# Masking the second attention behind its exponential on GpSimd, and a new order of steps

## The reference

```
x = x + L0_attention(norm(x), ctx)          # 16 heads of 16, softmax, no mask
x = x + L0_ffn(norm(x))                     # one of 8 experts, chosen by a gate
x = x + L1_attention(norm(x), ctx)          # 16 heads of 16, with cantor_mask:
    mask = cantor_mask(S, 7, 64)            # fixed pattern, 256 x 256, the same for all heads
    scores = q @ k.T * SCALE
    scores = where(mask, scores, finfo.min)
    attn = softmax(scores); out = (attn @ v) @ Wo + bo
x = x + L1_ffn ... L2_attention ... L2_ffn ... L3_attention ... L3_ffn
```

## Time and profile before

| | |
|---|---|
| runs | 987.82, 987.9, 988.53 us; median 987.9 |
| profiled execution, first to last instruction | 986.1 us |
| median of the runs less this span | 1.8 us |
| TensorE | busy 949.3 us (96%), mean granted clock 0.993 |
| VectorE | busy 634.1 us (64%) |
| ScalarE | busy 536.3 us (54%) |
| GpSimd | busy 221.5 us (22%) |

### The profile page before, as it was taken

How to read it: one execution, slowest core, us unless ns; L and a number is a source line. 1 busy time by engine, 2 the same in 40 slices (tenths; PEclk the granted TensorE clock), 3 DMA queues, 4 the chain that set the end, 5 groups by cost and what they waited for, 6 DMA issues and landing times.

```text
span 986.1 us, 17493 instructions
## 1 busy us (share of the span) xinstructions
PE 949.3 (96%) x6126; PEld 702.7 (71%) x6126; DVE 634.1 (64%) x2245; ACT 536.3 (54%) x1097; POOL 221.5 (22%) x317
## 2 busy tenths in 40 slices
PE   8999999989999999999999999999999999999998
PEld 6665665757687766778687766776686757777777
DVE  4634674675675776867586776775776676736564
ACT  1341644776368643875448644866376544864421
POOL 3104311303240132403141023302321032012210
PEclk9999999999999999999999999999999999999999
DMA  7308535400540023520432104402132004000000
GB/s 261 58 30 226 127 113 113 88 10 17 113 94 9 11 50 70 113 49 13 80 73 46 44 1 86 98 11 49 27 67 59 12 17 92 1 12 1 1 1 22
DMA packets 41078, 58.27 MB, mean 59 GB/s; under 512 B 4096, under 2 KB 35840, under 8 KB 37376
## 3 DMA queue, kind: packets, MB, share of 16 engines
q1 hardware_dynamic: 39600, 48.59, 23.6%
q10 hardware_dynamic: 1392, 8.56, 2.3%
HBM read 41.67 MB, written 13.89 MB: 56 GB/s over the span
## 4 chain that ended last, share of the span: by engine, by line
PE 77%; ACT 9%; DVE 8%; issue 4%; POOL 1%; DMA 1%; ACTq 0%; SPq 0%; DVEq 0%; POOLq 0%
PE bank L1657 11%; PE bank L1984 6%; PE bank L1517 6%; PE bank L1736 6%; PE bank L1714 6%; PE bank L1508 6%; PE bank L1629 4%; PE bank L1995 4%; PE bank L1771 4%; PE bank L1765 3%; PE bank L1717 3%; ACT PT L886 2%; ACT QA L873 2%; PE bank L1797 2%; PE bank L1526 2%
## 5 line engine op out<-in xcount | busy, mean ns | idle before, releaser
L886 ACT ACTIVATE PT<-bank 128x512 f32<-128x512 f32 x256 | 153.0, 598 | 127.4 <-PE bank L1717 71.8
L1657 PE MATMUL bank<-w,xhT 128*128 128x512 f32 x256 | 126.8, 599 | 0.0
L1714 PE MATMUL bank<-QA,KA 104*128 104x256 bf16 x512 | 112.7, 273 | 12.4 <-ACT PT L886 10.5
L1184 DVE CUSTOM_DVE_ANT_0 bank<-bank,maskb 128x256 f32<-128x256 f32 x256 | 101.7, 450 | 25.7 <-PE bank L1629 25.4
L1177 DVE TENSOR_REDUCE mx<-bank 128x2 f32<-128x512 f32 x128 | 83.6, 684 | 28.9 <-PE bank L1629 28.5
L1629 PE MATMUL bank<-KA,QA 96*128 96x256 bf16 x512 | 91.1, 273 | 1.9 <-DVE mx L1184 0.8
L1984 PE MATMUL bank<-xhBT,wi 128*128 128x256 f32 x336 | 87.0, 390 | 2.9 <-DVE hT L1491 2.5
L1714 PEld LDWEIGHTS bank<-QA,KA 104*128 104x128 bf16 x512 | 46.5, 99 | 60.3 <-issue 45.8
L1230 DVE SCALAR_TENSOR_TENSOR x<-bank,one,x 128x256 f32<-128x256 f32 x128 | 61.5, 481 | 21.6 <-PE bank L1657 17.6
L873 ACT COPY QA<-bank 8x256 bf16<-8x256 bf16 (+1 forms) x128 | 67.8, 575 | 10.1 <-PE bank L1695 8.8
L1984 PEld LDWEIGHTS bank<-xhBT,wi 128*128 128x128 f32 x336 | 59.2, 191 | 12.9 <-DVE hT L1491 5.6
(11 more groups left out here) (311 smaller groups left out, 2028.3 us busy)
## 6 DMA issues: line engine op xcount, KB each, us to landing
QA<-scratch SPq DMA_DIRECT2D x90, 128.0 KB, 4.8
scratch<-kparts SPq DMA_DIRECT2D x30, 192.0 KB, 2.4
KA<-scratch SPq DMA_DIRECT2D x15, 384.0 KB, 4.6
scratch<-qparts SPq DMA_DIRECT2D x30, 192.0 KB, 2.3
KA<-scratch SPq DMA_DIRECT2D x15, 256.0 KB, 5.5
w<-pack ACTq DMA_DIRECT2D x1, 2345.0 KB, 8.3
wi<-ipack ACTq DMA_DIRECT2D x1, 2304.0 KB, 8.5
xin<-x_in SPq DMA_DIRECT2D x8, 256.0 KB, 6.3
```

Of the source, the lines that this page charges most:

```text
L886: act.activation(PT[:, n % RING, :, :].rearrange("p t s -> p (t s)"), st_bank[:, :], ACT.Exp).then_inc(exp_s, 1)
L1184: last = dve.tensor_tensor_reduce(s, s, maskb[:, t, :], op0=ALU.add, op1=ALU.max, scale=1.0, scalar=-HUGE, accum_out=mx[:, i % 4, n % GH, ...
L1657: last = pe.matmul(bank[n % 2][:, :], xhT[:, kk, t * P:(t + 1) * P], W("exp0", KT)[:, kk, i * 512:(i + 1) * 512], start=(kk == 0), stop=(k ...
L1714: last = pe.matmul(st_bank[:, t * S:(t + 1) * S], KA[m][0:KM, v, t * P:(t + 1) * P], QA[m][0:KM, v, :], start=True, stop=(m == 0))
```

## The change

The 256 matmuls of L1717 go. For m = 1 the exponential is taken of unmasked scores. A new thread `value` on GpSimd waits for each head's exponential, multiplies the bits of the 128x512 weights, read as int32, by a tile `keepb` of int32 0 or 1, in place, and signals `kept_s`; the product with the values waits for `kept_s` in place of `exp_s` for m = 1. DVE makes `keepb` once, by two more 128x256 instructions, beside `maskb`. All five strings of `TURNS` are new. Per thread each engine still has the same number of letters, but for 128 new `v` on GpSimd, `w` 106 to 185 and `z` 54 to 56 on TensorE.

```diff
 TURNS = {
...
     "gpsimd":
-        "ppppppppssppsppsppsssppspssppsppssappsspsssasppaapapbbppbsbpsabssppbapbsaappsapbsbbspbpssabbbppssppp"
-        "apsapssaabbpspbbsbbsappssppaspbpassaaspbbbbbppsbapsaspspsppsspabasabpbbpbpabsbsbssappssssaaapbpssbss"
-        "bbbabaaasbabaabaabbaabaaaabcccccccccccccbc",
+        "ppppppppppppsssspppsppspssvsvpssvvvvvvpvvvvpvvvvsppsassapspppppsvvssvavvvaavvbvvvvbvbvvvpspbsasbpsbp"
+        "spppbpapavvvavsavvsvvbsvbbvvvvvvvbpsabsbsppsppppbspapaasavvvvbsvsvvbvpvvbvvbvvbvvsbappppbsasspppspvv"
+        "avvavsasvvvbsvbvbvvbvpvvvbsspbapbasspspppppsssvvavavavvvvbvpvbvvvvvvbbasbsbsspbspsvvsvspavvavavpvabv"
+        "vvsvvvvsbvssbbbabvvbvvvvvvvvvvvsvvvaaaabaaabbabaaabaabaccccccbcccccccc",
...
     "tensor":
-        "pppwwwppwwwwwwwwwwwwwwwwppwwwwwwwwwwwwpwwwwwpwpwwwwwwppwwwwwwwwwwwwwwwwwwwsswwspspssvsvswwvsvpsvswwv"
-        "ssvpvvssvpsvwwwvvvvwwvpvvvvwwwvpvwwwvvwwwwvpvwwvpvvpwwwwwwwpwspsssssssssssssssssppbspsspbsspssbpssvb"
...
+        "pppwwppwwwwwwwwwwwwwwwwwwwwwwwwppwwwwwwpwwwwwwwwwwwwwwwwwwwwwwwwpwpwwwwwppwwwwwwwwwwwwwwwwwwwwwwwwww"
+        "wwwwwwwwwwwwwwwwwwwwwwwwwwwwwwsswwspspssvwsvssvsvpvsswsvswvpvvpvsswwvwwvvvvwwvwwwwwvvvvpvwwvpvvwwvpv"
+        "wwvwwvvpwwwwwwwwwwspsssssssssspspssssssppwwwwwwwpspsswwwwwwwsspsspssvbsvbsbvssvwwwwpssvbsvbvpvvsspvb"
+        "vbvsvvvwwvpwvvvvbvwwvpvvssvpsvsssvwssvssvsssspsvsvpvvwwvwpwsvpsvsvvsvssvssvvvvssvsvvsvvsvssvsvssvpvp"
...
 }
@@ -208,6 +210,7 @@
         ident = W("ident")
         identb = sb("identb", [P, P], BF16)
         maskb = sb("maskb", [P, T, S], BF16)
+        keepb = sb("keepb", [P, T, S], I32)
         bqs = [sb(f"bqs{m}", [P, KT]) for m in range(3)]
         hb4 = sb("hb4", [P, 1])
         hb3 = sb("hb3", [P, 1])
@@ -364,7 +367,7 @@
 
         s_ps, max_s = sem("s_ps"), sem("max_s")
         mq_s, mT_ps, negm_s = sem("mq_s"), sem("mT_ps"), sem("negm_s")
-        st_ps, exp_s = sem("st_ps"), sem("exp_s")
+        st_ps, exp_s, kept_s = sem("st_ps"), sem("exp_s"), sem("kept_s")
         pv_ps, ot_s, otT_ps, att_s = sem("pv_ps"), sem("ot_s"), sem("otT_ps"), sem("att_s")
         attT_ps, attT_s, o_ps, added = sem("attT_ps"), sem("attT_s"), sem("o_ps"), sem("added")
 
@@ -694,6 +697,17 @@
                     plus(xb1, x, "bo1", xb1_s)
                     yield
 
+            def value():
+                pool.wait_ge(mask_ready, 3)
+                for q, (b, m) in enumerate(ATTENTIONS):
+                    if m == 0:
+                        continue
+                    for n in range(q * H, (q + 1) * H):
+                        pool.wait_ge(exp_s, n + 1)
+                        pt = PT[:, n % RING, :, :].bitcast(I32)
+                        pool.tensor_tensor(pt, pt, keepb[:, :, :], ALU.mult).then_inc(kept_s, 1)
+                        yield
+
             def net():
                 pool.wait_ge(w_in[6], 16)
                 for b in range(B):
@@ -748,7 +762,7 @@
             for m in range(2):
                 link("p", pool.memset(vflat[m][:, :, H * VW:], 0.0))
                 pool.memset(vaug[m][:, :, :, HD:HD + 1], 1.0).then_inc(ones_ready, 1)
-            weave("gpsimd", prep(), score(), iter(()), net(), rest(stream), rest(final))
+            weave("gpsimd", prep(), score(), value(), net(), rest(stream), rest(final))
 
 
         @block.scalar
@@ -1266,7 +1280,8 @@
                 yield
                 dve.wait_ge(nomask_in, 16)
                 for t in range(T):
-                    last = dve.tensor_copy(maskb[:, t, :], att[:, t, :])
+                    dve.tensor_copy(maskb[:, t, :], att[:, t, :])
+                    last = dve.tensor_scalar(keepb[:, t, :], att[:, t, :], 0.0, None, ALU.is_ge)
                 last.then_inc(mask_ready, 1)
                 yield
                 for q, (b, m) in enumerate(ATTENTIONS):
@@ -1700,7 +1715,7 @@
                     if q == 0:
                         pe.wait_ge(mask_ready, 1)
                     elif (b, m) == (0, 1):
-                        pe.wait_ge(mask_ready, 3)
+                        pe.wait_ge(mask_ready, 2)
                     tops(q, 0)
                     yield
                     for v in range(H + 4):
@@ -1712,10 +1727,7 @@
                                 pe.wait_ge(exp_s, n)
                             for t in range(T):
                                 last = pe.matmul(st_bank[:, t * S:(t + 1) * S], KA[m][0:KM, v, t * P:(t + 1) * P],
-                                                 QA[m][0:KM, v, :], start=True, stop=(m == 0))
-                                if m == 1:
-                                    last = pe.matmul(st_bank[:, t * S:(t + 1) * S], identb[:, :], maskb[:, t, :],
-                                                     start=False, stop=True)
+                                                 QA[m][0:KM, v, :], start=True, stop=True)
                             last.then_inc(st_ps, 1)
                             yield
                             if v % GH == 1 and v // GH + 1 < ITEMS:
@@ -1731,7 +1743,10 @@
                                     pe.wait_ge(attT_s, q)
                             for g in (2 * pair, 2 * pair + 1):
                                 i = q * ITEMS + g
-                                pe.wait_ge(exp_s, GH * (i + 1))
+                                if m == 0:
+                                    pe.wait_ge(exp_s, GH * (i + 1))
+                                else:
+                                    pe.wait_ge(kept_s, b * H + GH * (g + 1))
                                 for t, h in itertools.product(range(T), range(GH)):
                                     last = pe.matmul(pv_bank[32 * h:32 * h + 32, g % 2 * S:(g % 2 + 1) * S], vflat[m][:, t, (g * GH + h) * VW:(g * GH + h) * VW + 32],
                                                      PT[:, (i * GH + h) % RING, t, :], start=(t == 0), stop=(t == T - 1),
```

More of the change, by code:

```diff
@@ L90 @@
     "sync":
-        "pppppppppppppppppsssppbspppppppppppspssppsppppppppppbsssppsppbpppppppppsppsbspsppbpppppppppppbspspsp"
-        "spbpppppppbpppsppspssbppppppppsbsppspspppbpppspsssbcbbcc",
+        "pppppbpppppppppppspspssppppppppppppppsspspsppppppppppsppsspsppbbpppppppppbsppspsspbppppppppbppspspss"
+        "pppppppppbppspsspppbspppppppbpspsppssbpppppbppcssssbbbcc",
     "gpsimd":
-        "ppppppppssppsppsppsssppspssppsppssappsspsssasppaapapbbppbsbpsabssppbapbsaappsapbsbbspbpssabbbppssppp"
@@ L97 @@
+        "vvsvvvvsbvssbbbabvvbvvvvvvvvvvvsvvvaaaabaaabbabaaabaabaccccccbcccccccc",
     "scalar":
-        "pppppppppppvvpvvvpvvvvvvpvvvvvvvvvvvpvpsspsppsbsbpvpvbvvvpvvvvvvpvvvvvvvvsvvvvpbpvbvbbvvvsvbvvvvbvbv"
-        "vvvvvvbbvbpvvvvbpsbpasbabavavabvvvpvavpvvvvaapvvvvvpvavbvbvavvapvapvaavsavvvvvvvvavbavvvvvvbvpbvvvvb"
-        "vppsbsabbavaabavbpvavvpbvabvvvvvbpavbvvvvabvvavvvavpavaaabvvvvvavavpvvvpvsvvbvbvvvvvbvvvbvpbbspapsab"
-        "avavabvvvpbvpvabvvvavbavpbvvvvbavavvvavpavaaavbpvpavvavvsvpvvvvbvbvvbvvvvvpvbvvbvbvpssbababpavpbavbv"
@@ new lines @@
+        "pppppppppppvvpvvvpvvvvvvpvvvvvvvvvvvpvspsspppsssvbvpbvpvvpvvbvvvvpbvbbvvvvvvvvbvbvvbppvvvvvbsbvvvpvv"
+        "vbbvvvvvbvbvbvvbbvvbppvssaappavavbavvvavvpvvvaaavpvavvvvvbvvvvavavpapvavsavvvvvvavvavpvvvvvbvvvbvvvb"
+        "ppvsbsabbaavavabvvavbppvabvapbvvvbvavpbvavvvvbvavvvvaavabavvvvpvavavpvvvsvvvbvvvbvvvbvvvbvbbpsppasba"
+        "avavbavvpvpabvpvabvvvbvaavbvvavvbvvavvpvavaavabpvpvavavvsvvpvvvbvbvvvvbvvvvpbvpvbvbvsbsababvappbavbv"
+        "vapvbvvvabvvvavvavvavabvpvavvvavavapavvpvvvvvavavvsvbvbvpvvvbvvvbvvbvbpvpssbababavavabvvvavpvpvvvpvb"
@@ new lines @@
+        "avbvvvvabavavvvavpvabavavavsvvvvvavvavvvvvvbvvbvvvpbvvvbpabbasaspbabvppavbvvvvbvavvvvbvvvvvbvavbvvap"
+        "avavvapvvbvvvavsvaaavvvvaavvvvvbvvvvbsvsvbvcbabbaavavbavvvbavvvbvvababavabvvvavvbvavavavabvvaavbaaba"
+        "aaabaaaaaaaaaaaaabaaaaaaaaaaabbaaaabcbccbcbccbbcbccccccccccccccccccc",
+    "vector":
+        "ppppppvppvvppppppssssssssssssssssssssvvpvvppvsssspsspssssssspssssssppssssssssssssbssvbvpsvsssvspssss"
+        "psssssvssssssspspsssssvvsssssvvsvaasppsssssspssssaaassssssssssssssssssavssaassssvpvsvspssspvsspaaasp"
+        "aasasaabsbvsbsbbsbvbsbbssvsvbbbvaabsssppssbsbsssbssaaapssbssbsssssbssbssssbssaaavsbsbvssvvsspssvaaaa"
+        "abpsasspssabsapbsbssbvbbbbbbvsbssbsbvsvbpssvsababbssssspsspsssbapaasssbsssbssbssssbssavbsaasssssvssb"
+        "ssvsvspssaaaspaavpsabsspababpsbbsbbbbbbsvssbbsbsvsbvsvsbbsbvapapsssbpssssbssbsssbssaaabssssbsssssssb"
+        "vssaaasssvsspvbvssspsvpsaaasaapassspbasabsbsbsbbbbbbsvsbbsbsbsvssvvsbbvabasssssbsspsssbssspaaabssssp"
+        "sssssbssbsssvsbsssvaaasssssbsvsvssvsbsaaaaasasbsasabpbvsbvbbbpbbbsspvbvbsbvaabsspspbbbsssssbssssssss"
+        "bsaaasssbssbspvbssbssssssvaasasvsvsbsssvsssssssssbaaaassasabssaabsbsvssbbbbbvbbpvvbbbvacabcsssssbsbs"
+        "sbsssaaasbsssbsbsbssasaabbvvbaaaaababvvaabvabaaabbbbbbbaaaabbbaaaabaaaaaaaaaabbaaabcacccbccccccbcccc"
+        "cbcccbcccccbcbccccccccccccccccccbcccc",
```

43 lines of the change are left out of this document (14 added, 29 removed).

## The result

The changed kernel takes 1067.4 us in the median of 4 runs, the kernel before 987.9: a ratio of 1.0805, 95% interval [1.0781, 1.0828]. The prediction said 976.5 and at most 991. It is wrong by 91 us and in its sign.

The account below looks back on a forecast made before the run. It took TensorE's queue to bound the stretch from attention 1 to 15, and step order the first 135 us. 986.1 + 11.5 + 1.0 - 28.2 + 5.0 (stalls) - 0.7 = 974.7 of span, plus 1.8 outside: 976.5 us; range 965 to 991.

Parts of the forecast that it names:

- The 56 surplus spins: Ahead of the first scores: added spins cost 12.2 us, 0.7 absorbed by idle time, so +11.5 (bounds 11.0 to 12.3).
- The 22 others: Attention 1's stretch: 22 added spins, 4.8 us against 3.8 us of idle, forecast +1 (bounds 0 to 4.8).
- The transfer into `QA`: Before the first scores: transfers had landed by 35.48 us, so the scores would not have waited for them anyway.
- The multiplication's duration: GpSimd's 128 integer products of 128x512: 1.17 us each taken from the nearest rows, 150 us in all.
- Its use in TensorE: Masked attentions, heads 4 to 7: waits for the product in six of eight, 6 x 0.12 = 0.7 us.
- rival B: Masked attentions: the GpSimd product is slow; at 2.33 us each, 60 us lost, about 1036 us. Chance 0.15.
- the lock: GpSimd holding DVE instructions: 9.6 us before, 12 us more of DVE time, a quarter on the path: 3 us.
- rival C: Gain goes into queues: all 12 us of lock on the path, 5 us of held norms: 990 or 987. Chance 0.13.
- what is taken out of it should come back nearly whole: Stretch from attention 1 to 15, bound by TensorE's queue: removing 256 mask matmuls of 0.11 us gives -28.2 us.
- The lower bound of 14: Masks' removal on TensorE: about 14 us gained if the order behind it does not use half of it.
- the new order is the old one with the masks gone and 79 spins: Strings counted by milestone: other threads at the same steps, give or take three; the spins fall in the first 135 us.
- Clock: -0.7: Attention 1's stretch: a fall to half speed costs about 1.4 us; added spins there prevent half of one.

Follow-up runs that it names:

- the kernel before with spins: Kernel before plus 78 spins, 56 ahead of the first scores and 22 in attention 1's stretch: 999.4 us, ratio 1.0106.
- the narrow multiplication: Changed kernel with each multiplication cut from 128x512 to 128x16, most of the mask not applied: 1011.1 us; in the old order of steps 980.9 us.
- masks kept: Changed kernel's order with mask matmuls back on TensorE, plus a GpSimd multiplication behind each masked exponential that no engine waits for: 1051.4 us, ratio 1.0644.
- halves, old order: Change in the order of steps of the kernel before, each multiplication split into two of 128x256: 1053.8 us, ratio 1.0662.
- the new order: Changed kernel's order of steps; run alone, with mask matmuls back on TensorE and no multiplication: 1023.8 us, ratio 1.0369 to the kernel before.
- the old order: Order of steps of the kernel before; with the change, whole multiplications woven into GpSimd's old string: 1059.1 us, ratio 1.0745.
- unread multiplications: Masks gone, `keepb` times itself (128x512) per head on GpSimd, TensorE waiting for the exponential alone: new order 1054.0 us, old order 1025.6 us.
- four writes: Changed kernel with each multiplication replaced by a GpSimd memset of the same weights: 1033.9 us, ratio 1.0462.

## Why the prediction was wrong

**Right, and measured apart.** The 56 surplus spins (+11.5): first scores at 46.69, first stretch +10.9, and 11.8 in the kernel before with spins. The 22 others cost 2.3 there, where 1.0 was forecast. The transfer into `QA` had landed by then; the prediction left open how closely. The multiplication's duration, 1.17 taken, 1.28 measured. Its use in TensorE (0.7 us of waits): 0.8. So rival B did not come about, though no other rival had a time as long (1036, with products of 2.33 us): products were not slow.

**The step that failed first: the lock, 12 us on DVE, a quarter of it on the path.** Measured: DVE's excess is 53 us above the narrow multiplication's (67.7 - 14.5), and the time 56 us. Both factors were off, 12 us and a quarter.
*The size*: I scaled what the instructions of before had suffered by GpSimd's busy time. The estimate for before was fair (over the groups of `xhB`, `xh`, `xhA`, `mq` and `o`, count times mean less median makes 12 us against my 9.6), but 128 multiplications of 164 us do 53 us of harm where some 100 instructions of 120 us did 12. They run where DVE has its small steps, and behind 14 of the 68 `rstd` a multiplication is next in GpSimd's queue at the very moment when DVE starts on the norm. There it is not chance who meets whom; these 14 are some 12 us of it, and why the rest met so often was not taken apart.
*The share on the path*: "DVE is busy for 64%, a quarter on the path" read idle time as slack. In the masked attentions each small DVE result is waited for by TensorE, and in this pair of kernels a us of delay cost about a us of time. Between the other pairs it is 0.7 (masks kept: 42 us of excess, 27.6 of time) to 1.8 (halves, old order: 41 and 73, with the late products in it), so this is no fixed price. The earlier trace rows had all that was needed for the mechanism; rival C had it too, but capped at the same 12 us, so the range ended at 991 (its two terms on top of 976.5 are 990.5, given as 990).

**The step that failed second: "what is taken out of it should come back nearly whole", -28.2.** It came back as 12.7 us in the new order and 5.8 in the old, with the narrow multiplications in both. A stretch with 2% idle was not bound by TensorE alone: in the old order's masked attentions its busy time fell by 17.1 us and its idle time rose by 11.3. That other chains set the pace then is how I read it. The lower bound of 14 was closer and still too high.

**The step that failed third: "the new order is the old one with the masks gone and 79 spins".** Counted at the ends of attentions this holds, but the order of steps within them costs 24.4 us where the masks stay on TensorE (with whole multiplications, new and old order differ by 8 us, spins and all). This was not in the sum or the range at all.

**Clock: -0.7.** It went the other way, up to +29. The prediction priced falls of before, and had no term for falls that new idle time brings.

In the medians the whole is: 987.9, +11.5 spins, +24.4 order, -12.7 masks, +42.9 unread multiplications, +13.4 for their being read and 0.23 us longer = 1067.4. Each term holds for this order of adding and to some 4 us; by way of the old order it is 987.9, to 980.9 without masks, +45 unread, +33 read, +8 for the new order and its spins.

**What stays open.** Idle time and clock were not taken apart: no run held one fixed. That falls follow idle time is what the traces show in order of time. Of the 13.4 us the two causes were not separated. No run had the masks gone and nothing in their place, so what they are worth by themselves is known only together with the narrow multiplications. Which of the moved steps cost the 24.4 us was seen for 14.6 of them and tested for none. That the old order's remaining 33 us are the waits for products rests on a trace and a proportion, not on a run of its own.

## What to carry to other kernels

Before work moves to an idle GpSimd, look through DVE's groups for instructions whose longest is a GpSimd instruction long though their median is not, and ask which of them will start just as the new work does: a DVE step that waits for a GpSimd result met the next instruction of GpSimd's queue in all 14 cases of the change. Price such a hold at its full length, once per meeting, and as TensorE's time where TensorE waits for DVE; here that came to 0.7 to 1.8 us of time per us of hold. Price removed work by a run that all but removes it: here it gave 0.6%, which decides the matter before the replacement is even written. And spins are free only while they fill a wait: 19 taken out ahead of the first scores gained nothing, 78 put in, 17.0 us, cost 11.5.

## What the runs showed that I had not expected

- A GpSimd instruction of little over half the length, issued twice, did three quarters of the holding: DVE's excess is 60.7 us with 128 instructions of 1272 ns, 46.4 with 256 of 735 (old order).
- An integer product of 128x512 with both inputs the same tile takes 1.05 us, with two tiles 1.28.
- Doing the masking on the busier engine, DVE (766 ns each), was 35 us faster than on the idle one.
- A DVE instruction can be held over several GpSimd instructions in a row: 3.68 us over four writes, where a multiplication never held one for longer than itself.
- 7.9 of 12.2 us came back when 56 spins were removed from the change: the first stretch then has 2.7 us more of idle time, and a fall of the clock.
